# A routed mixture-of-experts layer on one core: expert rows added into the output by the scatter, all shared blocks beside the routing

## The reference

```
scores = softmax(xf @ gate_w.T)                 # xf: 4096 tokens x 256, layer-normed; 8 experts
top_vals, top_idx = top_k(scores, 2)
h = xf @ W1[e].T ; y, g = split(h)              # per expert, 192 wide
expert_e = (y * silu(g)) @ W2[e].T
z = sum over the two chosen e of top_val_e * expert_e
z = z + shared_mlp(xf)                          # the same gated MLP, 384 wide, for every token
x = x + tanh(g_ffn[1]) * z
```

## Time and profile before

| | us |
|---|---|
| median of three runs | 1096.27 |
| lowest and highest run | 1092.83, 1097.7 |
| the profiled execution's own time | 1098.07 |
| its span, first to last instruction | 1096.3 |
| PE busy | 962.1 (88% of the span) |
| DVE busy | 776.9 (71%) |
| ACT busy | 575.6 (53%) |
| POOL busy | 355.6 (32%) |

### The profile page before, as it was taken

The page is one execution under the profiler, slowest core; times in us unless marked ns, Lnnn a source line. Parts: engine busy times, 40 slices in busy tenths (PEclk is TensorE's granted clock), DMA queues, the critical chain, the costliest instruction groups (busy, mean ns, idle before and its releaser), DMA issues. The chain is left out here.

```text
span 1096.3 us, 22536 instructions
## 1 busy us (share of the span) xinstructions
PE 962.1 (88%) x6381; PEld 811.3 (74%) x6381; DVE 776.9 (71%) x2237; ACT 575.6 (53%) x1349; POOL 355.6 (32%) x551
## 2 busy tenths in 40 slices
PE   4999999999996679999999999854888889999973
PEld 3667666676764358999999999844777779999862
DVE  3677777777752436888888888855766658888767
ACT  1588888878884423443444434316355266556520
POOL 1011111111110013453444534422776514444410
PEclk9999999999998859999999999986989899999996
DMA  6776758576700400010010100201433214444267
GB/s 164 153 147 146 152 119 161 118 159 139 167 1 23 132 26 25 26 50 25 25 50 25 44 31 25 74 1 48 128 124 102 92 54 125 130 126 127 85 221 239
DMA packets 85873, 104.40 MB, mean 95 GB/s; under 512 B 15070, under 2 KB 75438, under 8 KB 85808
## 3 DMA queue, kind: packets, MB, share of 16 engines
q1 hardware_dynamic: 77616, 81.91, 30.4%
q0 software_dynamic: 7632, 21.05, 5.4%
q10 hardware_dynamic: 560, 0.66, 0.2%
HBM read 38.50 MB, written 57.62 MB: 88 GB/s over the span
## 5 line engine op out<-in xcount | busy, mean ns | idle before, releaser
L1604 POOL DMA_INDIRECT expert_out<-early_weights,aim x71 | 69.9, 985 | 101.6 <-DVE aim L1933 57.7
L1142 ACT ACTIVATE f_hidden<-c_hidden,f_b 128x256 f32<-128x256 f32 x128 | 53.7, 471 | 68.2 <-PE c_hidden L1331 68.2
L1595 POOL DMA_INDIRECT sorted_rows<-m_z,slot_i x64 | 71.8, 1122 | 44.4 <-DVE slot_i L1813 26.6
L1329 PE MATMUL c_mlp<-f_w_hi,f_hidden_hi 128*128 128x256 f32 x256 | 80.7, 315 | 3.6 <-DVE f_hidden_lo L1260 3.6
L1329 PE MATMUL c_hidden<-y2T_hi,f_w_hi 128*128 128x256 f32 x256 | 77.1, 301 | 0.0
L1331 PE MATMUL c_mlp<-f_w_hi,f_hidden_lo 128*128 128x256 f32 x256 | 72.4, 283 | 0.0
L1330 PE MATMUL c_mlp<-f_w_lo,f_hidden_hi 128*128 128x256 f32 x256 | 72.4, 283 | 0.0
L1331 PE MATMUL c_hidden<-y2T_hi,f_w_lo 128*128 128x256 f32 x256 | 72.2, 282 | 0.0
L1330 PE MATMUL c_hidden<-y2T_lo,f_w_hi 128*128 128x256 f32 x256 | 72.2, 282 | 0.0
L748 PE MATMUL ps_probT<-ident,prob 128*77 128x128 f32 x512 | 68.8, 279 | 3.8 <-ACT prob L479 3.3
L596 DVE TENSOR_REDUCE mx<-ps_scores 128x8 f32<-128x616 f32 x64 | 50.9, 796 | 28.0 <-PE ps_scores L682 27.9
(11 more groups left out here) (334 smaller groups left out, 3093.5 us busy)
## 6 DMA issues: line engine op xcount, KB each, us to landing
sorted_rows<-no_row SPq DMA_DIRECT2D x15, 2322.0 KB, 13.4
m_z<-sorted_rows SPq DMA_DIRECT2D x71, 129.0 KB
early_weights<-expert_chunks SPq DMA_DIRECT2D x8, 640.0 KB, 4.2
combT<-combineT_all SPq DMA_DIRECT2D x16, 256.0 KB, 2.3
slT<-slots_all SPq DMA_DIRECT2D x16, 256.0 KB, 2.5
early_weights<-expert_out SPq DMA_DIRECT2D x8, 512.0 KB, 6.3
early_weights<-expert_out POOLq DMA_DIRECT2D x8, 512.0 KB, 6.2
out<-x_all SPq DMA_DIRECT2D x8, 512.0 KB, 3.4
```

The source lines that it names most:

```text
L1142: last = act.activation(hf[:, q % 2, j, :], psH[:, q % 2, j, :], ACT.Relu, bias=fb1[:, c_:c_ + 1])
L1329: pe.matmul(out, lh, rh, start=start, stop=False, skip_group_check=shared)
L1595: pool.indirect_dma_start(out=sorted_rows[:, :], in_=zn[:, s % 3, t, :], in_offset=None, out_offset=bass.IndirectOffsetOnAxis(ap=slot_i[:, ...
L1604: pool.indirect_dma_start(out=expert_out[:, :], in_=xo[:, i % 3, :], in_offset=None, out_offset=bass.IndirectOffsetOnAxis(ap=aim_i[:, i % ...
```

## The change

In phase d:

- All eight blocks of the shared MLP run beside the routing: three units a step, two in step 0 and one after the last, 24 in all. `FIRST`, `LAST` and `TURN` go.
- The softmax weights are worked out in stage 1, block by block, and travel in two more columns of each sorted row (`ROW` from 258 to 260). ACT computes a tanh, DVE turns it to an exponential by `weights(s)`, nine small instructions of which each waits for the one before; `weights(s)` stands ahead of `places(s)`.
- SP writes each shared block with its residual to the output as soon as it is complete (`base_out`).
- `x_out` multiplies the tile by its rows' weights. POOL scatters it with `compute_op=ALU.add` straight into the output. Rows of no token go to 128 spare rows ahead of the output (the output tensor has 128 rows more, which the host cuts off).
- A token's second row may not be added while its first is on the way. The scatter of tile i waits for that of tile i-3 always, and for those of i-1 and i-2 where the tile's expert differs from the last tile's or the tile is past the used ones (a word of bits, `turns_i`, made in `tile_table`), and wherever i-1 or i-2 is below 6.
- There are six `xo` buffers in place of three, and twelve destinations and weights.
- Stage 3 is gone: no six units, no read back, no `combine`.
- The router's matmul streams 8 columns in place of 128 (120 of them were zero).

```diff
-            return [u for u in range(2 * s - 1, 2 * s + 1) if u >= 0] if s < NBLK else list(range(2 * NBLK - 1, BESIDE))
+            return [u for u in range(SC * s - 1, SC * s + 2) if 0 <= u < CHUNKS]
+        def added(eng, i):
+            eng.wait_ge(xo_out[i % XO].sem, 16 * (i // XO + 1))
...
 # sync
+            def base_out(b):
+                sp.wait_ge(res_done.sem, b + 1)
+                sp.dma_start(Y[:, b], X[:, b]).then_inc(o_out.sem, 16)
...
+                if e >= 4:
+                    base_out(e - 4)
+            for b in range(NE1 - 4, NBLK):
+                base_out(b)
             for j in range(3):
                 sp.wait_ge(sent[j].sem, 16 * 2 * BT * len(range(j, NBLK, 3)))
             sp.wait_ge(table.sem, 3)
...
 # gpsimd
+            pool.wait_ge(o_out.sem, 16 * NBLK)
+            pool.wait_ge(table.sem, 4)
             for i in range(XT):
+                if i % 16 == 0:
+                    word = pool.value_load(turns_i[0:1, i // 16:i // 16 + 1], min_val=0, max_val=2 ** 20 - 1)
                 pool.wait_ge(aim_done.sem, i + 1)
                 pool.wait_ge(xo_ev.sem, i + 1)
-                pool.indirect_dma_start(out=expert_out[:, :], in_=xo[:, i % 3, :], in_offset=None,
...
+                if i >= 3:
+                    added(pool, i - 3)
+                turn = (word >> (i % 16)) & 16
+                for k in (i - 1, i - 2):
+                    if k >= XO:
+                        pool.wait_ge(xo_out[k % XO].sem, turn + 16 * (k // XO))
+                        alone(pool)
+                    elif k >= 0:
+                        added(pool, k)
+                pool.indirect_dma_start(out=self.out[:, :], in_=xo[:, i % XO, :], in_offset=None, compute_op=ALU.add,
+                                        out_offset=bass.IndirectOffsetOnAxis(ap=aim_i[:, i % AIMS:i % AIMS + 1], axis=0))\
+                    .then_inc(xo_out[i % XO].sem, 16)
...
 # scalar
+            def tanh(f):
+                need(act, weight_step, f, 1)
+                act.activation(th[:], topd[:], ACT.Tanh, scale=1.0 / 8).then_inc(tanh_done.sem, 1)
...
-                if i >= 3:
-                    act.wait_ge(xo_out[i % 3].sem, 16 * (i // 3))
-                act.copy(xo[:, i % 3, :], xY[:, i % 2, 0, :]).then_inc(xo_ev.sem, 1)
+                act.wait_ge(aim_done.sem, i + 1)
+                if i >= XO:
+                    added(act, i - XO)
+                act.mul(xo[:, i % XO, :], xY[:, i % 2, 0, :], weight[:, i % AIMS:i % AIMS + 1]).then_inc(xo_ev.sem, 1)
...
 # vector
+            def weights(f):
+                done = weight_step.sem
+                last_two = zn[:, f % 3, :, D + 2:D + 4]
+                dve.wait_ge(tanh_done.sem, f + 1)
+                dve.tensor_scalar(odds[:], th[:], -1.0, 1.0, ALU.mult, ALU.add).then_inc(done, 1)
+                need(dve, weight_step, f, 2)
+                dve.reciprocal(odds[:], odds[:]).then_inc(done, 1)
...
                 if s < NBLK:
+                    weights(s)
                     places(s)
```

More of the change, by code:

```diff
@@ L1482, in phase_d @@
         rungs = early[:, 3 * D + XT * NE1:3 * D + (XT + NT) * NE1].rearrange("p (e n) -> p e n", n=NT)
[L1483 removed]
+        turned_flags = early[:, 12 * D:12 * D + 16 * XF].rearrange("p (g k) -> p g k", k=16)
         psG, psU = self.ps(c, "m_gate", [P, 2, TB]), self.ps(c, "m_up", [P, 2, TB])
@@ L1589, in _ @@
             rstd(1)
+            for k in range(16):
+                pool.memset(bits[:, k:k + 1], float(2 ** (k + 4)))
             for s in range(NBLK):
@@ L1682, in _ @@
                     zf_out(s + 1, 1)
-                    if s + 1 in FIRST:
-                        z_hi(s + 1)
+                    z_hi(s + 1)
+                if s < NBLK:
+                    tanh(s)
                 hidden_hi(first)
@@ L1692, in _ @@
                     expert_hi(s + 1)
-            act.wait_ge(sent[2].sem, 16 * 2 * BT * 2)
-            apply(LAST[0], 2).then_inc(zn_done.sem, 1)
-            act.wait_ge(table.sem, 3)
-            act.activation(topd[:], topd[:], ACT.Exp).then_inc(gate_exp.sem, 1)
             def x_zhi(i):
@@ L1736, in _ @@
                     x_out(i - 2)
-            def z_turned(q, k):
-                j = len(FIRST) + q
-                act.wait_ge(zt_mm.sem, 2 * NBLK + 2 * q + k + 1)
-                act.copy(zh[:, j % 2, k, :], (psT[:], psR[:].rearrange("p t q -> p (t q)"))[k]).then_inc(zh_done.sem, 1)
-            z_turned(0, 0)
-            z_turned(0, 1)
-            for m in range(BESIDE, NBLK * SC):
-                silu(m)
-                hidden_hi(m)
-                if m == BESIDE:
-                    z_turned(1, 0)
-                    z_turned(1, 1)
         @block.vector
@@ L1828, in hidden_lo, with result @@
                 dve.tensor_tensor(hl[:, m % 3, :], hf[:, m % 2, :], hh[:, m % 3, :].bitcast(F32), ALU.subtract).then_inc(hl_done.sem, 1)
-                if m % SC == 0 and m not in (0, BESIDE):
+                if m % SC == 0 and m:
                     result(m // SC - 1)
-            def result(j):
-                b = TURN[j]
-                dve.wait_ge(dn_mm.sem, (j + 1) * SC)
+            def result(b):
+                dve.wait_ge(dn_mm.sem, (b + 1) * SC)
                 for h in range(2):
@@ L2030, in logits @@
                     for k in range(KD):
-                        last = pe.matmul(psR[:, t, :], zf[:, k, t * P:(t + 1) * P], router[:, k, :], start=(k == 0), stop=(k == KD - 1))
+                        last = pe.matmul(psR[:, t, 0:NE1], zf[:, k, t * P:(t + 1) * P], router[:, k, :], start=(k == 0), stop=(k == KD - 1))
                 last.then_inc(r_mm.sem, 1)
@@ L2091, in _ @@
                     down(m - 1)
-                if not others:
-                    logits(s + 1)
-            down(BESIDE - 1)
+            down(CHUNKS - 1)
             pe.wait_ge(table.sem, 3)
             pe.wait_ge(wel_done.sem, NE1)
-            pe.wait_ge(res_done.sem, len(FIRST))
+            pe.wait_ge(res_done.sem, NBLK)
             pe.wait_ge(place_done.sem, 4 * NBLK)
@@ L2167, in _ @@
             pe.wait_ge(xo_ev.sem, XT)
-            def turn_last(q):
-                pe.wait_ge(zn_done.sem, NBLK + q + 1)
-                if q:
-                    pe.wait_ge(zl_done.sem, len(FIRST) + q)
-                for k in range(KD):
-                    for t in range(BT):
-                        out = psT[:, t * P:(t + 1) * P] if k == 0 else psR[:, t, :]
-                        last = pe.transpose(out, zn[:, 2 - q, t, k * P:(k + 1) * P], ident[:])
-                    last.then_inc(zt_mm.sem, 1)
-            turn_last(0)
-            for m in range(BESIDE, NBLK * SC):
-                up(m)
-                if m == BESIDE:
-                    turn_last(1)
-                else:
-                    down(m - 1)
-            down(NBLK * SC - 1)
 def spread(ap, dim, n):
```

185 lines of the change are left out of this document (79 added, 106 removed).

## The result

The changed kernel takes 1133.84 us (median of four runs, 1130.29 to 1139.89) against 1095.88 for the kernel before: a ratio of 1.0355, interval 1.0304 to 1.0405. Its profiled execution took 1134.04 us with a span of 1132.3, 36.0 more than before. The forecast was 1115.4 with a range to 1138: the sign and the range held, the size was half.

| kernel | phase d's first transpose | last `result` | first output copy | last output copy | span's end |
|---|---|---|---|---|---|
| before | 747.29 | 885.05 | 895.64 | 1039.23 | 1096.3 |
| after | 743.68 | 924.13 | 937.68 | 1105.40 | 1132.3 |
| grown by | -3.6 | 42.7 more | 3.0 more | 24.1 more | 30.2 less |

What follows compares the result with a forecast made beforehand. It took a DVE and ACT chain, as long as PE's work, to bound stage 1, and PE stage 2. Last copy 1039.2 + 44 + 3 + 11.7 = 1097.9, landing and end 1115.4; forecast median also 1115.4, range 1095 to 1138.

Steps and rivals of the forecast that it cites:

- Stage 1, +44: Routing with the shared MLP beside it: 44 us longer, 40 from longer steps and 4 from the clock; bounds +38 and +48.
- 18.5 and 0.6: One step of stage 1: 18.5 us of DVE and ACT operations in turn, plus thirteen hand-overs, making 19.1.
- +38: Lower bound of stage 1's growth in us: no clock loss and hand-overs half as dear.
- PE's pace: Rival, chance 0.10: stage 1's steps take PE's 15 to 17 us, stage 1 grows only 14 to 22, end 1070 to 1093.
- The clock, 0.5 a step: Stage 1: stretches at PE's lower clock level in most steps add 0.5 us a step, 4 in all.
- Between the stages, +3: From the last `result` to stage 2: gathers queue behind the last `base_out`, first transpose at 4.2 us; bounds 2 and 5.
- h = 4.65: Stage 2: us from one scatter's start to the next that must wait for its landing; bounds 3.65 and 5.65.
- Stage 2, +11.7: Output copies: 8.2 us from the serial first scatters making copy 12 late, 3.5 for early and short experts.
- twice as long over an adding scatter: Stage 2 aside: POOL taking twice the 1.0 us shown for a scatter would come out like the dear addition.
- the dear addition: Rival, chance 0.14: waiting adding scatters start 5.65 us apart, copy 12 is 15.2 late, the tail 22.4, end 1136.
- The tail, 17.4: Kernel's end: five waits in a row from scatter 66 put the last addition's landing 17.4 us after the last copy.
- A table load: Rival, chance 0.04: silu and tanh in different ACT tables, two loads a step, 20.5 us over eight steps, end 1136.

Runs made afterwards that it cites:

- e2: Changed kernel with the tanh and the nine operations of `weights` left out of stage 1, one memset in their place (for timing only): 1133.36 us, ratio 1.0293.
- e5: Changed kernel with ACT's normed rows of block s+2 put ahead of the last shared unit of step s: 1115.30 us, ratio 1.0185.
- e1: Changed kernel with stage 2's scatter writing its rows in place of adding them, all waits kept (for timing only): 1120.34 us, ratio 1.0169.
- e3: Changed kernel with the first six tiles' scatters freed of the extra waits where their expert has not changed: 1122.63 us, ratio 1.0202.
- e4: Changed kernel with padding rows in four sets of spare rows and no wait flags on the empty end tiles: 1128.79 us, ratio 1.0242.
- e12: e10 with the last `base_out` ahead of the first gathers again: 1087.54 us, ratio 0.9918.
- e9: Changed kernel with four edits: first six tiles free, padding rows in four sets, normed rows sooner, first gathers ahead of the last `base_out`: 1099.83 us, ratio 0.9982.
- e10: e9 with `tile_table` one shared unit later on DVE in the last step of stage 1: 1094.56 us, ratio 0.9926.
- e11: e10 with nine output buffers and sixteen sets of aim and weight: 1097.25 us, ratio 0.9946.
- e7: e9's four edits on the changed kernel, plus `weights` computed later on DVE: 1107.72 us, ratio 1.0110.

## Why the prediction was right or wrong

- **Stage 1, +44: right in size (the stage grew 42.7), wrong in its reason, so the size was luck.** The failed step is the sum of 18.5 and 0.6 "from one `rows_in` to the next, on DVE and ACT by turns". Its 19.1 met the measured 19.3 to 20.0 only because a second loop is about as long. The true one is PE's unbroken 15.7 us, then silu, hidden, high part and rows, 4.1 us. PE's "between 15 and 17" was right; that these 4.1 come on top of it was missing. e2 took 2.1 us from the first loop and gained 0.8 a step, all of it clock; e5 opened the second and gained 3.3 to 4.0. And e5, with every operation of the list still there, has steps of 16.0: they don't have to follow one another for 19.1 us. That the same sum gave 12 to 13 for the kernel before, with 13.4 measured, made me trust it; two lists of about the same length can't be told apart by their length. The chain view of the kernel before had both loops. One turns through PE, from its first transpose to the silu and the rows: the steps from 798.98 (14.5 us) and 813.49 (12.4). The next step is my list, from `expert_hi` to the next transpose, 13.7 us:

```profile
813.49 0.66 PE m_turned L2022 x4
...
821.87 0.61 ACT silu L1659
...
823.95 1.97 ACT m_z L1631 x4
825.92 1.16 ACT x_weights_hi L1624
...
839.60 0.66 PE m_turned L2022 x4
```

  I read the second and put the new unit on it alone. The lower edge that I kept "without any clock loss", +38, was no bound for that reason: with the order of e5 stage 1 grows by 24.2 us, just over the upper edge of the rival PE's pace (22), whose condition, a chain at least 2 us shorter than the list, e5 meets.
- **The clock, 0.5 a step: low.** Steps of this loop with a stretch at the lower level lose 0.9 to 1.6 us by it (18.4 without it in e2; 19.3 to 20.0 with it in after and e2).
- **Between the stages, +3: right** (+3.0), first transpose 4.1 us after `result` where 4.2 was said. After is the lowest of the nine kernels with this order of SP's queue, though: last `result` to first copy is 13.6 us here and up to 16.2 in e5, and 10.6 before.
- **h = 4.65: right at the end (4.63 to 4.69), a little low elsewhere** (4.96 on average at the start, 4.89 at the changes of expert). Its make-up was not what I took: of the 1.43 over a plain write's 3.24 in e1, 0.59 is POOL's own and 0.84 the landing. (The Trainium skill, DMA: Bandwidth & Descriptors, "Latency and other measured facts", has 0.2 us for an HBM access on average and 2 at high load: the 0.84 lies between, and the choice of one of the two would have been wrong.) With 0.2 in place of 1 my own terms give 9.6 us less (seven and five hops of 0.8), not the 8 that I wrote.
- **Stage 2, +11.7: wrong, +24.1.** The failed step is "after that three in flight need h/3 = 1.55 a tile, under 2.07". POOL itself needs 1.55 + 0.30 = 1.86, since the scatter that adds takes it 0.59 longer. At 0.2 us a tile the backlog of the serial start was still 10 us when the third change of expert came, where I had it given back at 0.5. I had written that POOL "twice as long over an adding scatter" would come out like the dear addition, and gave it no part in my own sum. Copy 12 came 9.9 late against PE's pace of 2.09 (8.2 was said), by the longer first hops. How much each is worth is an estimate: lay the kernel's waits out tile by tile, with 2.07 us a tile on PE, h = 4.65 and the changes of expert where the trace has them, and the copies take 153 us with 1.26 us between free scatters (e1's), 160.5 with 1.86, and 164 with the hops as measured at the start and the changes; measured are 167.7. So POOL's own time is some 7 of the 12.4 that were missing and the hops some 3.5. The rest is not shown; landings in dense stretches may be it (copy 28 got its buffer 5.6 us after the scatter's start, copy 12 after 3.9).
- **The tail, 17.4: wrong, 26.9.** The hops are right (four of 4.67). Scatter 66 starts 7.25 us after its copy and not 1.24, again POOL's lag, +6.0 (the estimate above has 8.5 with 1.86 us between scatters and 1.5 with 1.26); from the last scatter's start to the end are 8.5 us and not 3.85, +4.7, most of it the stretch in which nothing moves; the copies of tiles 67 to 70 took 7.5 and not 6.3, -1.2.
- **The sum.** -4.9 in stage 1 (3.6 of it the sooner begin of phase d), +12.4 in stage 2 and +9.5 in the tail are the 17 us between the forecast's end of 1115.4 and 1132.3. That the range held is in part luck too: its upper part was there for an h near 5.65, which no average shows. Of the rivals, the sentence on a POOL slower over an adding scatter came nearest, with 1136.
- **A table load: none.** In phase d of after the silu's table is loaded once and never for the tanh, which takes 0.22 us:

```profile
L1681 ACT ACTIVATE top_tanh<-top_under 128x32 f32<-128x32 f32 x8 | 1.8, 224 | 1.5 <-DVE top_under L1794 1.5
...
L1671 ACT ACT_TABLE_LOAD x1 | 1.3, 1283 | 0.0
```

- **Why stage 3's 57 us didn't come back.** 30.2 of them are saved at the end. Stage 1 took 42.7: six units on an engine that was busy there already (24.2 with e5's order, at PE's pace in its middle steps), and an order of calls on ACT that fitted two units and not three (18.5). The additions took 24.1 in stage 2, 15.6 of it for the waits of the first tiles (e3).

## What to carry to other kernels

Work that goes "beside" a stage costs its full time on the engine that sets the stage; follow the chain view around several whole periods, and put the new work on every loop that it shows, before a list of operations is summed, and after the work is added look again which call of the other engines should come first. A wait put in for the first laps, because it is easy there, can cost as much as one on every turn: where the queue behind it needs nine tenths of the pace, as here, it did not recover in 59 tiles. Price an unseen operation on the engine that issues it too, not only in its landing.

## What the runs showed of the hardware

- An indirect DMA of 128 rows of 1 KB with an addition takes GpSimd 1.553 us, without it 0.961; the next dependent one starts 4.67 and 3.24 us after it at the end of the stage, and 4.52 to 6.23 and 3.22 to 5.44 us earlier in it.
- The kernels that end on GpSimd's waits for scatters have over 4 us without any bytes or instructions at the end of the span (after, e1, e4, e12); the kernel before, which ends on a store by SyncE, has none. The cause is open.
- ScalarE began some instructions 1.7 to 2.9 us after their last input was done, released by nothing that the profile names but "remote" (e1, e9, e10, e11; none in the other runs; all four ran on the chip of e1 to e4, where e2 to e4 have none). Each such place in stage 1 costs a step 2.8 us. The Trainium skill, Runtime: NRT & Kernel Launch, "Instruction fetch mechanics", has code fetched by a DMA queue of its own, which could stall an engine; the queues that moved packets from 834 to 838 us in e9 speak against it here, there being none of instructions among them (nor in two more of the four stretches in e9; in the fourth, from 853.8 to 856.7 us, there is one packet):

```profile
q1 hardware_dynamic: 92, 0.47, 58.4%
q0 software_dynamic: 48, 0.13, 9.3%
```

  e12 lacks both the edit of the gathers and the stalls, but it also ran on another chip than e9 to e11, and e7 had that edit without stalls. The cause stays open.
